# Sixteen fields of chunk 1 by look-up, four each of chunks 2 and 3, and these two chunks' gathers begun eight tiles sooner

## The reference

```python
e = jnp.stack([tbl_0[ids[:, 0]], ..., tbl_38[ids[:, 38]]], axis=1)      # (512, 39, 16)
for W in (W0, W1):                                                       # both layers give 128 maps
    xk = jnp.einsum('bid,bjd,ijh->bhd', x0, xk, W.reshape(m, Hk, Hn))
    outs.append(xk)
z = jnp.sum(jnp.concatenate(outs, axis=1), axis=-1)
h = jnp.concatenate([z, dense_ctx], axis=1)
h = jnp.maximum(h @ W_top1 + b_top1, 0.0)
h = jnp.maximum(h @ W_top2 + b_top2, 0.0)
y = h @ W_top3
```

## Time and profile before

| what | us |
|---|---|
| median of 3 runs | 233.66 |
| lowest and highest run | 233.04, 234.36 |
| profiled execution, its device time | 232.75 |
| its span in the trace | 230.9 |
| busy: PE, PE weight loads | 214.8, 171.9 |
| busy: DVE, ACT, POOL | 164.6, 159.6, 98.9 |

### The profile page before, as it was taken

How to read it: one execution, slowest core, us unless ns; L and a number is a source line. 1 busy time by engine, 2 the same in 40 slices (tenths; PEclk the granted TensorE clock), 3 DMA queues, 4 the chain that set the end, 5 groups by cost and what they waited for, 6 DMA issues and landing times.

```text
span 230.9 us, 4818 instructions
## 1 busy us (share of the span) xinstructions
PE 214.8 (93%) x1717; PEld 171.9 (74%) x1717; DVE 164.6 (71%) x347; ACT 159.6 (69%) x319; POOL 98.9 (43%) x99
## 2 busy tenths in 40 slices
PE   4389799999499999999999999999999999999996
PEld 4378367676366578988787788887876788887995
DVE  3999997968678996877869986866587855561101
ACT  3996889799749786588685957787668575663201
POOL 4774687777447777750667777600000000000000
PEclk9979999999889999999999999999999999999999
DMA  4990029713000000000000000000000000000000
GB/s 125 257 293 6 17 67 296 193 25 80 4 7 9 7 7 6 9 6 0 9 6 6 10 6 9 6 1 3 0 0 4 0 0 3 0 0 3 0 0 3
DMA packets 7579, 8.57 MB, mean 37 GB/s; under 512 B 2631, under 2 KB 5164, under 8 KB 7556
## 3 DMA queue, kind: packets, MB, share of 16 engines
q1 hardware_dynamic: 4516, 7.48, 11.4%
q0 software_dynamic: 3040, 0.78, 3.6%
HBM read 8.25 MB, written 0.00 MB: 36 GB/s over the span
## 4 chain that ended last, share of the span: by engine, by line
PE 81%; ACT 5%; issue 4%; DVE 4%; DMA 3%; POOL 1%; SPq 1%; ACTq 0%; DVEq 0%
PE turn_bank L606 16%; PE x_bank L535 10%; PE pair_bank L507 9%; PE x_bank L538 8%; PE x_bank L537 8%; PE g_bank L569 5%; PE misc_bank L569 3%; PE g_bank L586 3%; PE turn_bank L644 3%; PE x_bank L549 3%; PE turn_bank L617 2%; DMA tab<-small 2%; PE pair_bank L734 1%; PE x_bank L743 1%; PE x_bank L524 1%
## 5 line engine op out<-in xcount | busy, mean ns | idle before, releaser
L477 POOL DMA_INDIRECT emb<-tbl,ids_sb x95 | 98.7, 1039 | 49.7 <-ACT prod L1046 25.7
L1046 ACT ACTIVATE prod<-pair_bank 128x512 f32<-128x512 f32 (+1 forms) x108 | 64.9, 609 | 39.6 <-PE pair_bank L507 39.6
L896 DVE TENSOR_TENSOR prod_lo<-prod,prod_hi 128x512 fp32r<-128x512 f32 x92 | 61.9, 686 | 10.1 <-ACT prod_hi L1051 9.2
L535 PE MATMUL x_bank<-prod_hi,pair_w_hi 128*128 128x512 f32 (+1 forms) x108 | 59.9, 555 | 1.1 <-DVE prod_lo L896 0.9
L507 PE MATMUL pair_bank<-x,sel 117*128 117x512 bf16 (+1 forms) x112 | 42.0, 384 | 1.2 <-ACT x L1024 0.7
L606 PEld LDWEIGHTS turn_bank<-g_sb,w_sb 128*128 128x128 f32 x312 | 40.0, 191 | 3.4 <-issue 1.0
L606 PE MATMUL turn_bank<-g_sb,w_sb 128*128 128x128 f32 x312 | 42.3, 278 | 0.0
L1051 ACT ACTIVATE prod_hi<-prod 128x512 fp32r<-128x512 f32 x64 | 41.1, 642 | 0.2
L538 PE MATMUL x_bank<-prod_hi,pair_w_lo 128*128 128x512 f32 x92 | 36.5, 397 | 0.0
L537 PE MATMUL x_bank<-prod_lo,pair_w_hi 128*128 128x512 f32 x92 | 36.4, 395 | 0.0
L884 DVE CAST prod_hi<-prod 128x512 fp32r<-128x512 f32 x44 | 18.6, 423 | 17.5 <-ACT prod L1046 17.4
(11 more groups left out here) (147 smaller groups left out, 306.4 us busy)
## 6 DMA issues: line engine op xcount, KB each, us to landing
emb<-tbl,ids_sb POOLq DMA_INDIRECT x95, 2.4
tab<-small SPq DMA_DIRECT2D x2, 560.0 KB
wt<-w_top SPq DMA_DIRECT2D x2, 512.0 KB
tab<-small SPq DMA_DIRECT2D x1, 504.0 KB
wa<-pair_w_a SPq DMA_DIRECT2D x1, 448.0 KB
wb<-pair_w_b SPq DMA_DIRECT2D x1, 448.0 KB
wtd<-w_dense SPq DMA_DIRECT2D x1, 256.0 KB
dense_sb<-dense_t SPq DMA_DIRECT2D x1, 256.0 KB
```

Source lines behind the costliest of these rows:

```text
L477: pool.indirect_dma_start(out=emb[:, at:at + D], out_offset=None, in_=tables[f], in_offset=bass.IndirectOffsetOnAxis(ap=ids_sb[:, c * M + ...
L535: mm = pe.matmul(x1_banks[k % 2][:, :], pair_w_hi[p, t, :], hi(n), start=(t == 0), stop=(t == FULL))
L896: dve.tensor_tensor(lo(n), prod[rows, n % RING, :], prod_hi[rows, n % RING2, :], ALU.subtract).then_inc(lo_done, 1)
L1046: act.activation(prod[0:ROWS[t], n % RING, :], pair_bank[n % 2][0:ROWS[t], :], ACT.Square).then_inc(sq_done, 1)
```

## The change

Four things change, and line numbers after them shift by 2 to 10.

- `PARTS = (0, 4, 1, 1)`: four parts (16 fields) are looked up for chunk 1, one part (4 fields) each for chunks 2 and 3. Gathers: 14 + 23 + 35 + 35 = 107. Look-ups: six. The slots of ids fall from 36 to 24, so that one instead of three later spreads of ids is left (`LATE_AT`).
- The look-ups of chunk 1 run at tiles 5, 9, 13 and 18 (`FIRST_LOOKS`); those of chunks 2 and 3 at tiles 39 and 67. The one-hot tiles of chunk 1 are placed by a rule of their own (`hot_step`).
- The gathers of chunks 2 and 3 may begin eight tiles sooner: the first may run when 20 tiles (48 tiles) are squared, where it was 28 (56).
- `later_looked` becomes a buffer of its own and no longer lies in `rest`.

```diff
-AHEAD_TILES, REST_TILES = 18, 4
+AHEAD_TILES, REST_TILES, LEAD_TILES = 18, 4, 8
...
-PARTS = (0, 3, 3, 3)
-LATE_AT = (NT + 1, 2 * NT + 3, 2 * NT + 5)
+PARTS = (0, 4, 1, 1)
+
+FIRST_LOOKS = (5, 9, 13, 18)
+LATE_AT = (NT + 1,)
...
-        later_looked = rest[:, 0:LATER * max(PARTS) * E].rearrange("b (f q d) -> b f q d", q=3, d=D)
+        later_looked = sb("later_looked", [128, LATER * max(PARTS), 3, D])
...
-            return ((c - 1) * NB + part + (c > 1 and PARTS[c] < 3)) * NT + LOOK_AT + (nth(c, part) == 0)
+            return FIRST_LOOKS[part] if c == 1 else ((c - 1) * NB + part + (PARTS[c] < 3)) * NT + LOOK_AT
...
+        def hot_step(c, part, r):
+
+            if c > 1:
+                return max(look_step(c, part) - 6 + r, (c - 1) * NB * NT)
+            begin = look_step(c, part - 1) if part else 0
+            return begin + (look_step(c, part) - 2 - begin) * r // (HOT - 1)
...
-                    if max(look_step(c, part) - 6 + r, (c - 1) * NB * NT) == n]
+                    if hot_step(c, part, r) == n]
...
-            part = AHEAD_TILES * (f - first) // (CUTS[1] - first) if f < CUTS[1] else (
+            lead = LEAD_TILES if c > 1 else 0
+            part = (AHEAD_TILES + lead) * (f - first) // (CUTS[1] - first) - lead if f < CUTS[1] else (
```

## The result

Over 22 runs of each kernel the changed one takes 232.99 us (230.43 to 235.7) and the kernel before 234.19 us (232.92 to 235.4): the ratio is 0.9931, with a 95% interval of 0.9907 to 0.9954. The ratio leaves out the four executions of the changed kernel that are over 1.5% above its fastest (233.9 to 235.7 us) and none of the kernel before, so it flatters the change a little: the two medians alone give 0.9949. On the scale of the table's 233.66 that is 232.05 us by the ratio and 232.5 by the medians; the forecast was 232.5, in a range of 229.6 to 235.2.

What follows compares the result with a forecast made beforehand. PE bounds except where POOL's 35 gathers end chunk 1: earlier gains shrink to 0.5 us, slow clock costs 1.0, chunk 2 saves 1.72; span 230.9 - 1.15 = 229.75 us, 232.5 on the median's scale, range 229.6 to 235.2.

Steps and rivals of the forecast that it cites:

- boundary 3 waits long (the rate is worse): Sign of being wrong: a long gather wait at the end of chunk 2, where at most 1 us was forecast.
- boundary 3: Start of chunk 3: first select at 159.1 instead of 160.24 us, with PE last by 0.7 us.
- 2.6 + 1.56 = 4.2: End of chunk 0: 2.6 us sooner without late gathers and two id copies, 1.56 more if the clock stays up.
- DVE's one-hot tiles: Chunk 0: five more on DVE, 1.9 us, counted at nothing because ACT ends last there.
- The rate of gathers: POOL, chunks 2 and 3: 34 intervals between 35 gathers take 46.1 and 45.7 us, from whole-chunk rates and 1.30 for seven.
- boundary 2: End of chunk 1: POOL's gathers hold the next first select to 111.3 us, 112.3 with the slow clock; 111.77 before.
- The rival of the faster POOL: Chunks 1 and 2: gathers shorten with fewer one-hot tiles or idle DVE, total 229.3 to 231.4 us; chance 0.15.
- the row at 40.46: Earlier trace: a gather took 0.95 us beside DVE's one-hot tile and rounding, so dropping one-hot tiles buys gathers nothing.
- the slower rival: POOL's gather rate worsens: tie from 0.02 us a gather, 235.0 us at 0.035 more, 236.4 at 0.05; chance 0.18.
- Landing and slack: Ends of chunks: a last gather is used 2.5 us after its start, select follows 5.9 later; 2.5 us are slack.
- The clock at boundary 2: End of chunk 1: PE's idle time brings the slow clock, 1.56 us in full, taken as 1.0.
- Two look-ups fewer: PE in chunks 1 and 2: each loses two look-ups at 0.86 us, 1.72 us per chunk.

## Why the prediction held, point by point

**The mechanism was right for chunks 0 and 1, not for chunk 2.** POOL runs unbroken from 55 to 154 us. Chunk 0 ends without waiting for a gather, chunk 1 ends when the 35 gathers have landed, PE idles there and the clock falls behind it. At the end of chunk 2, where I had PE last and at most 1 us of waiting, DVE waits 3.64 us for a gather: POOL is last there too. That is the sign of being wrong that the prediction had named, "boundary 3 waits long (the rate is worse)". The first select of chunk 2 comes 87.6 us after the first of all; 112.3 - 25.24 = 87.1 was forecast, 86.5 was before. Of what chunk 0 and the look-ups gained, 0.5 us was to be left there at the full clock; in the trace nothing is left, and the boundary comes 1.1 us later than before.

**Chunk 0: 3.1 us instead of 2.6 + 1.56 = 4.2.** The clock did stay up (0.46 us for five transposes at 61.60, against 0.76 in the earlier trace rows), and PE's idle time fell to 1.71 us, where I had 1.9. The missing us lies ahead of the transposes: ACT is free at 60.83 - 0.9 = 59.9, hardly before the 60.03 of before, though two copies of ids are gone. What ate it is likely the extra look-up on PE or DVE's one-hot tiles, which I had counted at nothing; no run takes the two apart. The kernel with 31 and 31 gathers shows how tight this stretch is: a second spread at tile 19 costs 0.5 us (38.5 against 38.0).

**The rate of gathers: 1.396 and 1.400 us, not 1.356 and 1.344.** From 57.05 to 104.53 are 34 intervals in 47.48 us where I had 46.1, and from 105.78 to 153.37 47.59 where I had 45.7. I had taken 1.067 and 1.050 us a gather from windows over whole chunks and had put seven intervals at 1.30. The unbroken row of 1.384 us, which the prediction quotes from the earlier trace rows, was the better figure: 34 intervals of it are 47.06. With it boundary 3 would have stood at 158.4 + 2.3 = 160.7, behind the 160.24 of before, and the forecast would have been no gain at all. The longest gather starts with DVE's `split_lo` and lasts through what DVE does next:

```profile
148.82 1.10 DVE L812 TENSOR_TENSOR parts<-rest 128x512 bf16<-128x512 f32 x1
...
148.88 2.78 POOL L487 DMA_INDIRECT emb<-tbl,ids_sb  x1 [0.30 <-issue]
...
149.79 0.46 DVE L894 CAST prod_hi<-prod 128x512 fp32r<-128x512 f32 x1
...
150.12 0.73 DVE L906 TENSOR_TENSOR prod_lo<-prod,prod_hi 128x512 fp32r<-128x512 f32 x1
...
150.71 0.54 DVE L926 COPY g_sb<-g_bank 128x320 f32<-128x320 f32 x1
...
151.12 0.54 DVE L926 COPY g_sb<-x_bank 128x320 f32<-128x320 f32 x1
```

It and the one at 98.61, which took 1.87 us beside the `split_lo` of the chunk before, are together 2.8 us above 0.94 each. In the kernel before a gather that starts with `split_lo` (99.61) took only 0.95, so the neighbour alone doesn't decide it, and why these two were so long stays open. The rate was the mis-sized term that mattered: 1.4 us at boundary 2 and 3.3 in sum at boundary 3. Two other terms took part of it back: POOL began chunk 2's gathers 0.65 us sooner than forecast (57.05 - 26.14 = 30.91 us after the first select, where 56.8 - 25.24 = 31.56 was forecast), and less stood behind the wait (the next paragraph). The rival of the faster POOL fell, and with it the thought that fewer one-hot tiles would speed gathers up, as the row at 40.46 had said. What happened instead is the mechanism of the slower rival, a worse rate, though not its time.

**Landing and slack: right.** From start to use 2.53 us (104.53 to 107.06, 153.37 to 155.90), 2.5 forecast. From use to select 5.19 us at the full clock; I had 5.9. So 3.2 us are covered at boundary 3, not 2.5.

**The clock at boundary 2: the wrong account.** I charged 1.0 us for it and passed that on to boundary 3, because I held PE to be last there by 0.7. At boundary 2 it cost 1.5 (6.67 us from use to select, against 5.19 at the full clock). At boundary 3 POOL was last, and the kernel with the extra matmuls shows that the clock's time is not on that path.

**Two look-ups fewer are worth 1.08 and 1.21 us, not 1.72.** The windows run from the first select of chunks 1 and 2 to the 22nd. First the kernel before, with three look-ups, then the changed one with one, then the kernel with 31 and 31 gathers and two:

```profile
66.31:97.32 31.01, 30.50 (x247) 1.00 0.07 7
111.77:145.79 34.02, 34.02 (x284) 1.00 0.07 8
...
64.13:94.06 29.93, 29.15 (x208) 1.00 0.07 7
113.73:146.54 32.81, 32.71 (x243) 1.00 0.07 8
...
63.90:94.64 30.74, 29.93 (x227) 1.00 0.09 8
109.09:142.74 33.65, 33.55 (x264) 1.00 0.08 8
```

From one look-up to two it takes 0.81 and 0.84 us more, nearly the 0.86 of PE's chain; from two to three only 0.27 and 0.37. So it isn't each look-up that is cheaper than I had it but the one that only the kernel before has, at tiles 32 and 60, early in the chunk. Where its cost is hidden I didn't find out; PE's idle time in the windows accounts for a small part (0.51 and 0 us before, 0.78 and 0.10 changed). This term gave 0.5 us too much in chunk 2.

**The sum.** In the traces the start of chunk 3 stands at 134.95 us from the first select, 133.8 was forecast and 135.0 was before. The forecast gain of 1.15 us is thus not in this pair of traces; in the medians it is 1.2 us. Executions of these kernels differ by 2 us and more, and these two lie on opposite sides of their medians. Where within the kernels the average gain falls can't be told from one trace each: 3.1 us in chunk 0 and the -4.1 in chunk 1 both vary with where the clock falls. So the cause of the small gain in the medians stays open; what the traces and runs show is why it isn't larger. The forecast number is right, and that it agrees so closely is luck: chunk 0 was overrated by 1.1 us, the look-ups by 0.5, and the time of POOL's gathers was underrated by 3.3. That is 0.036 us a gather over the 91 intervals ahead of boundary 3, and by the prediction's own reckoning 0.02 is a tie and 0.035 a loss of 0.5%.

## What to carry to other kernels

An engine at 43% of the span can be the bound: divide its work by the stretch in which it must be done. Here 35 gathers x 1.40 us = 49 us stand against chunks that PE alone would end in an estimated 44.4 and 47.3 us (the 45.5 and 48.5 of before less 1.1 and 1.2 for two look-ups). When work is moved from a saturated engine to one with slack, move only until the second one's stretch is full: 31 gathers instead of 35 for chunks 2 and 3 gave 0.9835 instead of 0.9931. Take the rate of such an engine from a stretch in which it runs without a pause, beside the work that it will meet. Where a late transfer can't be avoided, shorten what stands behind its wait: putting the split one and two tiles later brought chunk 3 forward by 1.7 us in the trace, though the times of that kernel don't yet tell it from the changed one.

## What I had not expected of the hardware

A gather's issue on POOL takes 0.94 us undisturbed and up to 2.78 us beside DVE's work, and it is the tensor_tensor instructions that go with the long ones. In the six traces from chips without pauses (the two kernels, 31 and 31 gathers, the extra matmuls, the later split, and chunk 1's part with spreads at tiles 19 and 20) 522 gathers start behind the 22nd us. The 29 that met no DVE instruction took 0.94 to 0.95 us, and the 44 that met DVE instructions but no tensor_tensor (one-hot tiles, casts, copies) 0.94 to 1.05. Of the 118 that met tensor_tensor alone 44 took more than 1.05 us, up to 1.68, and of the 331 that met both kinds 126 did, up to 2.78. One with tensor_tensor alone, in the kernel before:

```profile
115.50 0.69 DVE L896 TENSOR_TENSOR prod_lo<-prod,prod_hi 128x512 fp32r<-128x512 f32 x1
...
115.65 1.36 POOL L477 DMA_INDIRECT emb<-tbl,ids_sb  x1 [0.30 <-ACT prod L1046]
```

The Trainium skill (SBUF — State Buffer, Who interferes with whom) lets a tensor_tensor with two SBUF inputs hold up only GpSimd instructions that read SBUF, and infers that descriptor generation is not among what it stalls. The gathers stretch all the same; they take their ids from SBUF, so it may be that read which waits, and no run here tells. Nothing was run that isolates the pair.

The granted clock fell behind idle times of PE of 3.29 us, 2.55 us, and 1.93 us (in the kernel with spreads at tiles 19 and 20), and didn't fall behind 1.71 us.

Chips differ more than this change: the kernel before took 233.79 us on one and 264.94 and 265.01 us on two others, with pauses before instructions that wait for nothing, and there the order of the variants is another.
